# Slot attention with two row buffers in turn, and the first batch's maxima ahead of the last row statistics

## The reference, cut to what matters

```python
def _layernorm(x, axis=-1, eps=1e-05): ...
def _L0_ffn_ref(x, slot_query, ...):          # x: [8, 512, 512], already normalised; H = 16 heads, NS = 16 slots
    q = jnp.broadcast_to(slot_query, (Bx, NS, D))
    o = q + _mha(q, x, x, d_Wq, ...)          # slot attention: softmax(q k^T / sqrt(dh)) v, per batch and head
    h = _layernorm(o.reshape(Bx, E, S, D), ...) 
    u, g = silu(h @ e_W1 + e_b1), silu(h @ e_Wg + e_bg)   # 16 experts, one per slot, 4 MB per matrix
    o = o + (u * g) @ e_W2 + e_b2
    return _mha(x, o, o, c_Wq, ...)           # every row attends to the 16 slots
x = x + tanh(g_xattn) * _L0_xattn_ref(_layernorm(x), ctx, ...)
x = x + tanh(g_ffn) * _L0_ffn_ref(_layernorm(x), ...)
```

## Time and profile before

| | us |
|---|---|
| three runs of the kernel before: median (lowest to highest) | 2421.1 (2413.06 to 2422.67) |
| the profiled execution, its own time | 2415.6 |
| the span of its trace, first to last instruction | 2413.8 |

### The profile page before, as it was taken

One profiled execution on the slowest core, in us unless ns is written; L12 is line 12 of the kernel. 1 busy time (PEld: TensorE's weight loads), 2 busy tenths in 40 slices (PEclk: granted clock), 3 DMA queues, 4 the chain that ended last, 5 costly groups with the idle time before them and its releaser, 6 DMA issues. The chain is left out here.

```text
span 2413.8 us, 30028 instructions
## 1 busy us (share of the span) xinstructions
PE 2131.5 (88%) x11425; PEld 1592.4 (66%) x11425; DVE 1335.3 (55%) x2112; ACT 673.0 (28%) x1066; POOL 618.8 (26%) x552
## 2 busy tenths in 40 slices
PE   6999999999989999999999999998997527445898
PEld 5677777776767778888888888887873102111477
DVE  7665665556447777666766676666651000000377
ACT  2544564446533321212111212222420000000231
POOL 5444654355348850320032000000320000000010
PEclk9999999999999999999999999998997768677999
DMA  4223223311287659664966494434769999999857
GB/s 155 76 102 128 75 72 111 128 62 62 88 319 298 239 209 377 227 217 160 358 223 221 158 369 161 161 128 151 297 269 410 426 430 426 427 429 428 302 227 261
DMA packets 181397, 565.13 MB, mean 234 GB/s; under 512 B 15473, under 2 KB 98961, under 8 KB 152561
## 3 DMA queue, kind: packets, MB, share of 16 engines
q1 hardware_dynamic: 171952, 504.37, 55.4%
q10 hardware_dynamic: 9312, 58.99, 5.9%
HBM read 450.07 MB, written 113.25 MB: 233 GB/s over the span
## 5 line engine op out<-in xcount | busy, mean ns | idle before, releaser
L1446 PE MATMUL ff_down<-w,u 128*128 128x512 f32 x1536 | 360.8, 393 | 11.4 <-DVE ff_x L1720 10.2
L1386 PE MATMUL ff_up<-ff_t,w 128*128 128x512 f32 x1488 | 357.6, 389 | 0.0
L1446 PEld LDWEIGHTS ff_down<-w,u 128*128 128x128 f32 x1536 | 288.2, 189 | 78.0 <-DVE ff_x L1720 17.2
L1386 PEld LDWEIGHTS ff_up<-ff_t,w 128*128 128x128 f32 x1488 | 279.6, 188 | 58.1
L1720 DVE SCALAR_TENSOR_TENSOR ff_x<-ff_down,gates,ff_x 128x512 f32<-128x512 f32 x256 | 190.8, 748 | 85.5 <-PE ff_down L1446 83.6
L2474 PE MATMUL e_down<-e_w,e_ug 128*32 128x512 f32 x480 | 77.2, 802 | 180.9 <-DMA e_w<-in_L_ffn_e_W 180.9
L1386 PE MATMUL ff_up<-ff_b,w 128*128 128x512 f32 x960 | 235.8, 389 | 0.0
L1386 PEld LDWEIGHTS ff_up<-ff_b,w 128*128 128x128 f32 x960 | 180.2, 188 | 37.4
L2474 PEld LDWEIGHTS e_down<-e_w,e_ug 128*32 128x32 f32 x480 | 17.8, 142 | 239.0 <-DMA e_w<-in_L_ffn_e_W 190.7
L2576 DVE TENSOR_TENSOR e_u_rows<-e_turned,e_b1T 128x128 f32<-128x128 f32 x16 | 4.7, 291 | 264.6 <-PE e_turned L2465 264.6
L1511 ACT ACTIVATE ff_gate<-ff_gate 128x512 f32<-128x512 f32 x62 | 39.2, 633 | 400.2 <-DVE ff_gate L1696 400.2
(11 more groups left out here) (449 smaller groups left out, 4400.5 us busy)
## 6 DMA issues: line engine op xcount, KB each, us to landing
w<-ff_w_factors SPq DMA_DIRECT2D x48, 1792.0 KB, 7.4
e_w<-in_L_ffn_e_W SPq DMA_DIRECT2D x17, 4096.0 KB, 22.1
e_wg<-in_L_ffn_e_Wg SPq DMA_DIRECT2D x16, 4096.0 KB, 30.0
e_w<-in_L_ffn_e_W ACTq DMA_DIRECT2D x13, 4096.0 KB, 51.4
ff_w_factors<-w SPq DMA_DIRECT2D x15, 1792.0 KB, 7.0
w<-ff_w_parts SPq DMA_DIRECT2D x48, 512.0 KB, 5.7
ff_t<-ff_t_factors SPq DMA_DIRECT2D x16, 1024.0 KB, 13.9
ff_b<-xnT SPq DMA_DIRECT2D x11, 1024.0 KB, 11.0
```

The lines of the kernel that those rows point to most:

```text
L1386: last = nc.tensor.matmul(bank[:, :], a, m, start=start and c == 0, stop=stop and c == 5)
L1446: last = nc.tensor.matmul(DN[m % 2][:, :], a, w, start=c == 0, stop=c == 5)
```

## The change

There are now two row tiles: `y[0]` is the old `y_xin`, `y[1]` the old `y`, now called `y_odd`. Rows of batch b are loaded into `y[b % 2]` and normalised in place. With that:

- `norm(b)` no longer waits for POOL; instead the load into a tile waits until PE has turned and POOL has read what was in it.
- The rows of batch 1 are loaded on SP as soon as PE has made the queries (`BUILT["q"]`), not after `norm(0)`.
- On DVE `norm(1)` stands right behind the last `ff_x` tile, ahead of `maxima(0)`. The raw statistics of batch 7 and the mean and variance of batches 2 to 7 stand at the end of batch 0's turn in the loop. `refine` stands behind `maxima(1)`, ahead of `norm(2)`.
- On ACT the Ln and Exp of those variances stand behind `probs(0)`.
- SP's first two expert quarters wait on `rows_seen`, since their place covers `ff_x`.

```diff
-            see_rows(B - 1)
+            slot.see_last_rows = lambda: see_rows(B - 1)
...
-        y = mem.sbuf("y", [P, TT, D])
+        y = [xin, mem.sbuf("y_odd", [P, TT, D])]
...
         def load_rows(sp, b):
-            sp.dma_start(xin[:, :, :], x_v[b]).then_inc(x_in, 16)
+            sp.dma_start(y[b % 2][:, :, :], x_v[b]).then_inc(rows_in[b % 2], 16)
 
         def second_rows(sp):
-            sp.wait_ge(y_ready, 1)
+            sp.wait_ge(built, BUILT["q"])
             load_rows(sp, 1)
...
                 if b + 2 < B:
-                    sp.wait_ge(y_ready, b + 2)
+                    sp.wait_ge(yn_lo_done, b + 1)
+                    sp.wait_ge(g_ready, done("y", b, KT - 1))
                     load_rows(sp, b + 2)
                 if b + 1 < B:
                     keep(b + 1)
+                if b < 2:
+                    sp.wait_ge(rows_seen, B - 1 + b)
...
             act.wait_ge(down_ready, all_tiles)
             values(0)
-            act.wait_ge(kept, KEPT["other_variances"])
-            nc.scalar.activation(rstd[:, EARLY:], var[:, EARLY:], ACT.Ln)
-            act.drain()
-            nc.scalar.activation(rstd[:, EARLY:], rstd[:, EARLY:], ACT.Exp, scale=-0.5).then_inc(copied, 1)
             for b in range(B):
...
                 probs(b)
+                if b == 0:
+                    act.wait_ge(kept, KEPT["other_variances"])
+                    nc.scalar.activation(rstd[:, EARLY:], var[:, EARLY:], ACT.Ln)
+                    act.drain()
+                    nc.scalar.activation(rstd[:, EARLY:], rstd[:, EARLY:], ACT.Exp, scale=-0.5).then_inc(copied, 1)
...
         def norm(dve, b):
-            dve.wait_ge(x_in, b * 16 + 16)
-            if b:
-                dve.wait_ge(yn_lo_done, b)
+            dve.wait_ge(rows_in[b % 2], (b // 2 + 1) * 16)
             for t in range(TT):
                 n = b * TT + t
-                last = nc.vector.tensor_scalar(y[:, t, :], xin[:, t, :], mean[:, n:n + 1], rstd[:, n:n + 1], ALU.subtract, ALU.mult)
+                last = nc.vector.tensor_scalar(y[b % 2][:, t, :], y[b % 2][:, t, :], mean[:, n:n + 1], rstd[:, n:n + 1], ALU.subtract, ALU.mult)
             last.then_inc(y_ready, 1)
...
-            statistics(EARLY, B * TT)
+            norm(dve, 1)
             for b in range(B):
                 maxima(b)
-                if b == 0:
+                if b == 1:
                     dve.wait_ge(copied, COPIED["other_rstd"])
                     refine(rstd[:, EARLY:], var[:, EARLY:], half[:, EARLY:])
-                if b + 1 < B:
+                if 1 <= b < B - 1:
                     norm(dve, b + 1)
...
                 inverse(b)
+                if b == 0:
+                    see_last_rows()
+                    nc.vector.drain()
+                    statistics(EARLY, B * TT)
```

More of the change, by code:

```diff
@@ L1775, in vector @@
             residual(last_chunk - 1, range(5, TILES))
-            see_rows(B - 1)
+            slot.see_last_rows = lambda: see_rows(B - 1)
             v.drain()
-        return (sync, tensor, scalar, gpsimd, vector), (x_out, PAIRS * 16), (down_ready, down_taken, last_chunk * TILES)
+        return (sync, tensor, scalar, gpsimd, vector), (x_out, PAIRS * 16), (down_ready, down_taken, last_chunk * TILES, rows_seen)
 def slot_places(nc, stack, low_bytes):
@@ L1803, in __init__ @@
     def __init__(self, second_rows, turn_weights, make_queries, make_products, turn_first_rows, first_copies, first_statistics, keep_queries, keep_products, keep_first_rows):
-        self.second_rows = second_rows
+        self.second_rows, self.see_last_rows = second_rows, None
         self.turn_weights, self.make_queries, self.make_products, self.turn_first_rows = turn_weights, make_queries, make_products, turn_first_rows
@@ L1855, in slot_attention @@
         sq, bk_col, bq_col = (vectors[n] for n in ("sq", "k_col", "q_col"))
-        down_ready, down_taken, all_tiles = ff_down
+        down_ready, down_taken, all_tiles, rows_seen = ff_down
         mem.sbuf("vectors_place", [P, 18 * 256 + 576 + D + 2 * 8])
@@ L1866, in slot_attention @@
         gains_in = mem.sem("d_gains_in")
+        rows_in = [x_in, mem.sem("d_odd_rows_in")]
         y_ready, yn_hi_done, yn_lo_done, *yT_out = (mem.sem(f"d_{n}") for n in ("y_ready", "yn_hi", "yn_lo", "yT_hi_out", "yT_lo_out"))
@@ L1957, in turn_rows @@
                 for t in range(TT):
-                    last = nc.tensor.transpose(bank[:, t * P:(t + 1) * P], y[:, t, k * P:(k + 1) * P], ident[:, :])
+                    last = nc.tensor.transpose(bank[:, t * P:(t + 1) * P], y[b % 2][:, t, k * P:(k + 1) * P], ident[:, :])
                 last.then_inc(g_ready, 1)
@@ L2110, in values @@
                     act.wait_ge(g_ready, done("z", b - 2, 1))
-                nc.scalar.copy(yn[0][:, b % 2], y[:, :, :]).then_inc(yn_hi_done, 1)
+                nc.scalar.copy(yn[0][:, b % 2], y[b % 2][:, :, :]).then_inc(yn_hi_done, 1)
             def probs(b):
@@ L2145, in gpsimd @@
                 pool.wait_ge(yn_hi_done, b + 1)
-                nc.gpsimd.tensor_tensor(yn[1][:, b % 2], y[:, :, :], plain(yn[0][:, b % 2]), ALU.subtract).then_inc(yn_lo_done, 1)
+                nc.gpsimd.tensor_tensor(yn[1][:, b % 2], y[b % 2][:, :, :], plain(yn[0][:, b % 2]), ALU.subtract).then_inc(yn_lo_done, 1)
             pool.wait_ge(gains_in, (3 * B + 3) * 16)
@@ L2208, in keep_first_rows, with vector @@
             row_lows(dve, 0)
-        def vector(dve):
+        def vector(dve, see_last_rows):
             def prob_lows(b):
@@ L2309, in _ @@
                 ff_vector(dve, steps)
-                vector(dve)
+                vector(dve, steps.see_last_rows)
         return (first_w1, first_wg, first_w2, second_w2), w1_in, wg_in, w2_in
```

## The result

| | kernel before | changed kernel |
|---|---|---|
| median, us (lowest to highest of 20 executions each) | 2419.2 (2413.06 to 2424.96) | 2424.0 (2418.91 to 2432.67) |
| ratio of the changed kernel to before, 95% interval | | 1.0023 (1.0014 to 1.0032) |
| span of the profiled execution | 2413.8 | 2419.8 |

The change makes the kernel slower, by 0.23% or 5.6 us (3.4 to 7.7). The forecast was +3.5 us, as a time 2424.6.

The account below looks back on a forecast made before the run. It took PE to bound slot attention and transfers the experts behind it. Batch 2's later turns (+1.1) and the lower clock (+2.4) made +3.5 us on 2421.1, forecasting 2424.6, range 2412 to 2431.

Parts of the forecast that it names:

- The bound: PE bounds slot attention, transfers the experts behind it: a microsecond before the last score moves the end by one.
- The price of the stop: PE's 6.08 us stop ahead of batch 1's turns, a 0.68 wait and 2.4 for the clock: at most 9.2 us.
- Step 2: `norm(1)` on DVE: its fourth instruction, held by POOL's `yn_lo`, ends at about 1681.05, against 1676.55 if free.
- Steps 3 and 4: Batch 0's maxima and copies: PE waits 1.2 us for `exp(0)`; `score(1)` starts at 1687.4, gaining 4.2 us.
- Step 5: Put-off statistics on DVE: last variance starts at 1692.8; `score(1)` takes 5.58 us, ends at 1693.0, so maxima hardly wait.
- second rival: Clock falls already between 1681 and 1687, `score(1)` ends late, a tiny DVE instruction is held: +5.0 us, chance 0.10.
- Step 6: POOL's `yn_lo(1)`, 0.25 us ahead, holds `norm(2)`; batch 2's turns start at 1701.95, 1.1 us later than before.
- S: Start of the last variance instruction (L2153) on DVE, forecast at 1692.8, from which the race with POOL is timed.
- Step 7: PE's 5.9 us stop ahead of batch 2's turns halves the clock: 4.97 us in place of 2.60, 2.4 more.
- First rival: `norm` isn't held by POOL, or wins the race: -4.4 us, or -3.3 if only `norm(1)` is held; chance 0.28.
- Third rival: Batch 2's rows load late, so the change frees nothing: price up to 8 us, chance 3 in 100.

Follow-up runs that it names:

- pool_waits_0: Changed kernel, but POOL starts `yn_lo` of batch 0 only when `norm(1)` is done; ratio to before 1.0035, run once more 1.0030.
- after_again: The changed kernel run once more, with no edit; ratio to before 1.0019, stretch 118.58 us.
- before_filled: Kernel before, with 48 identity transposes on PE in its stop ahead of batch 1's turns; ratio to before 0.9992.
- after_filled_2: Changed kernel, with 44 identity transposes on PE in its stop ahead of batch 2's turns; ratio to before 1.0011, stretch 115.76 us.
- after_filled_all: Changed kernel, with 44 identity transposes ahead of batch 2's turns, 8 ahead of `turn_probs(0)` and 16 ahead of `score(1)`; ratio to before 1.0002.
- pool_waits_both: Changed kernel, but POOL's `yn_lo` of batches 0 and 1 waits until the next batch is normalised; ratio to before 1.0000, stretch 111.65 us.
- pool_waits_1_filled: Changed kernel, but POOL's `yn_lo(1)` waits for `norm(2)`, and 8 and 16 transposes fill the two stops ahead of `score(1)`; ratio to before 0.9990.
- two_buffers_old_order: Changed kernel's two row tiles, loads and SP waits, but DVE and ACT in the order of the kernel before; ratio to before 0.9996.
- early_store: Changed kernel, POOL waiting at batches 0 and 1, batch 0's turned rows stored ahead of the last `ff_x` store; ratio 0.9984, with two fills 0.9986.

## Why the prediction was right, and where it was not

**The bound.** The stretch grew by 4.7 us, the median by 4.8, the ratio says 5.6 (3.4 to 7.7). That what moves the last score moves the end fits this, and fits the table of the experiments in the main; pool_waits_0, with 7.3 to 8.5 us for 3.1 to 4.4, is the exception. One trace can't show it to the microsecond: from the first expert matrix to the end it was 626.3 us before, 625.1 in the changed kernel and 628.9 in after_again. The prediction held that no change under 0.5% could be told; with twenty executions each the interval was 0.09% to either side, and the loss is clear of it.

**Luck in the time.** The forecast of 2424.6 lies 0.6 us from the measured 2424.0. It started from 2421.1, the median of three executions, where twenty gave 2419.2; that 1.9 us covered the 1.3 us by which the growth was too small.

**The price of the stop.** "At most 9.2 us" counts 2.4 us for the clock at batch 1, taken from the difference to batch 2. before_filled shows that 1.1 of them could be had there, as PE waits for the row lows next. The forecast itself uses the 2.4 us at batch 2 only, where after_filled_2 measures them.

**Step 2, `norm(1)`, right.** Forecast: the fourth instruction is held and ends at 1681.05. It took 4.82 us from 1678.47 on, 0.24 behind POOL, and ended at 1683.30 - 2.45 = 1680.85. That a one-input instruction from SBUF to SBUF is held, for which the prediction had one cast, now stands on 6.20 us in the six traces in which POOL's instruction starts beside `norm(1)`, against 1.91 or 1.92 in the eight others. The Trainium skill (GPSIMD Engine Reference, Key points) names contention with VectorE's 2-port modes. The trace agrees with it; no row here tells which port it is.

**Steps 3 and 4, right.** PE's wait for `exp(0)` is 1.18 us (forecast 1.2), and `score(1)` starts at 1687.16 (1687.4).

**Step 5, the failed step: the length of `score(1)`.** The last variance starts at 1694.96 - 2.45 = 1692.51 (1692.8). But "`score(1)` takes 5.58 and ends at 1693.0" took the length from the earlier trace rows, where it ran at full clock. It took 7.2 us and ended at 1694.4, past 1693.6, the point that the second rival names as the one from which the tiny instruction is held.

**Step 6, right in place and size, wrong in what was held.** POOL came at 1697.56 - 1694.96 = 2.60 behind S, as forecast. `L2224` came at S + 2.82 and was held instead of `norm(2)`. As the chain from there to `norm(2)`'s end follows POOL, the turns of batch 2 started at 1702.83 and not 1701.95: +0.9 us. after_filled_all, with `score(1)` at full clock, shows the forecast's own path.

**Step 7, right.** From the first turn to the sums of batch 2 it is 1710.32 - 1705.28 = 5.04 us instead of 2.60: +2.4, as forecast.

The sum by its steps: +2.0 (1702.83 against 1700.79) and +2.4 make +4.5, where the forecast had +1.1 and +2.4; the last 0.2 of the 4.7 us come behind batch 2's sums. That is the second rival's path but for the moment at which the clock fell: not in 1681 to 1687, where PE had little to do, but from 1688.3 on in before's terms, inside matmuls without a gap. It came back at 1691.3, near the 1691 of the rival. Its price came out close, +4.5 against +5.0. I gave it 0.10, too little: the argument against it, that turns alone hadn't lowered the clock between 1700 and 1703, looked at work and not at the stops between it.

**First rival, wrong.** It needs a `norm` that isn't held; when POOL stands aside the stretch is 2.1 us shorter than before (pool_waits_both), not 4.4, since `score(1)` is slow then too. With the clock held up it is 3.4 us shorter (pool_waits_1_filled), and there `norm(1)` is still held: that is the -3.3 that the rival gave for this case.

**Third rival, wrong.** No instruction of `norm(2)` waited for its rows. They landed at 1690.54, 7.4 us behind their issue, and `norm(2)` came at 1703.31.

## What to carry to other kernels

Before an order is changed, look at which instructions it kept apart. Here the wait that was taken away cost nothing alone (two_buffers_old_order); the new order put POOL's 4.6 us instruction beside DVE's short ones, and whoever comes 0.2 us too late stands for all of it. When work is moved forward on one engine, move what it collides with on the other too; one wait on POOL turned +4.7 us of the stretch into -2.0 (the ratio, 0.9984 to 1.0005, doesn't tell that gain from none). And spread-out stops aren't free because they are short: several of 1 to 3 us can cost the clock just as one of 6 us does, and a length read at full clock is then the wrong term.

## What the hardware showed that I had not expected

- The clock can fall behind stops, in the midst of dense work. After stops of 0.5, 1.2 and 2.0 us it fell 1.1 us into `score(1)` and stayed low for some 3 us. In all eight traces of the changed order in which the last two stops weren't filled it fell, 0.7 to 1.6 us into `score(1)`, also behind stops of 1.0 and 2.0 to 2.8 us alone. In all three in which they were filled it stayed at 1.00 there.
- Transposes alone kept the clock up: 44 in 4.96 us, and the 16 turns behind them in 1.97. They also brought it back: behind the stop of 5.49 us in pool_waits_0 PE did nothing but turns, at 0.50 from 1703 to 1705, and its 8 transposes at 1706.40 took 1.04 us, as at full speed.
- The low clock of batch 0's end moves between executions. In the trace it is 0.68 and 0.64 in the two stretches from 1655 to 1665 and full in `score(0)`; in before_filled and both early_store kernels the first matmuls of `score(0)` took 0.76 to 0.77 us instead of 0.47. It makes `score(0)` 2.2 us longer, and what decides it isn't shown by any run here.
- An instruction on 128 x 2 lasted 4.33 to 4.36 us beside POOL in five traces: the price of the hold is POOL's rest, not the size of DVE's instruction.
- The hold goes both ways. In the six traces in which POOL's instruction started within the third one of `norm(1)` it took 4.78 or 4.79 us; otherwise, for batches 0 to 2, 4.54 to 4.61.
